# Two-layer perceiver kernel on one Trainium2 core: norm weights, value bias and attention denominator applied at a later point, four chunks of the last convolution as products on TensorE

## The chip, the cores and the metric

The kernel runs on one core of a Trainium2 chip. A core has a matrix engine (TensorE, PE in the profile), a vector engine (DVE), a scalar engine (ACT), GpSimd (POOL), and a queue for transfers (SyncE, SP). Each engine works through its own list of instructions in order, and waits on semaphores where it needs another engine's result. The metric is device time of one launch in microseconds (us); lower is better.

## The reference

The inputs are x (1×128×256), a context (1×12544×256) and a mask (1×128×12544). All arithmetic is float32. Cut to what is computed:

```python
# layer 0
x = x + xattn(layernorm(x), ctx, mask)       # 16 heads of 16, q, k, v with biases
#   scores = (q/4) @ k.T + (1-mask)*-10000; softmax; @ v
n = (x - mean) * rsqrt(var + 1e-5) * ln1_w + ln1_b
Q, K = elu(n @ q_w.T + q_b) + 1, elu(n @ k_w.T + k_b) + 1    # 64 features
V = n @ v_w.T + v_b
attn = causal(Q @ K.T) @ V / (causal(Q @ K.T) @ 1 + 1e-6)
# (then o_w, o_b, a residual, a norm with ln2_w and ln2_b, gelu FFN 256-1024-256)
# then an FFN with gate, 256-1024-256: activations rounded to 8 bits, weights to -1, 0, 1
# layer 1
x = x + (xattn(layernorm(x), ctx, no mask) @ Wo.T + bo)
# then an RWKV time mix (decay scan), and the last FFN:
h = bit_linear(norm(x), w1)                              # 128 x 1024
h = silu(conv3(h, conv_w) + conv_b)                      # per channel, 3 taps along the sequence
x = x + bit_linear(h, w2)
```

## The kernel before

The order of every engine is written out by hand. A layer's cross-attention goes over the context in NB = 14 blocks of TILES = 7 tiles of 128 keys. The 28 blocks are numbered m = 0 to 27; the program's step (m, t) is tile t of block m.

For each block TensorE makes the keys (`keys_in`, L1252, four units) and values (`values_in`, L1242), a rough maximum of the scores in bf16 (`maximum`, L1259, 32 products a block), the scores (L1315 brings in minus the maximum, L1319 the products of q and k), and the weighing of the values (`weigh`, L1337). In layer 0 DVE takes each maximum with the mask (L916) and adds the mask to half of a tile's scores (L977); ACT copies the other half to SBUF (`copy_second`, L652), POOL adds the mask there (`add_bias`, L500), and ACT takes the exponential of each (L659). In layer 1 there is no mask, ACT takes the exponential from PSUM (L664) and POOL is nearly idle.

The new running maximum of a block must come to rows before the next block's scores can use it: TensorE turns it (`turn_max`, L1354), and ACT copies it (`rows_out`, L638). This is done in the last step of a block, t = 6 (ROWS_AT). In steps like these `lent(m, t)` gives a product a bank of the scores' own: at t = 6 `turn_max` writes into a bank that is lent from the scores, ps_scores, which is free only when DVE has added the mask to it (L977); it stands behind the weighing and one pair of maxima, and ahead of the next unit of keys. In block 0, step 2, the small product L1487 uses the lent bank in the same way. How many maxima stand at each step comes from `count_at`, which bank each uses from the table MAX_BANK; `late_bank(m, t)` says at which steps of layer 0 the maximum behind the scores goes to ps_proj rather than ps_max.

Between the layers lies a part that I call the middle: end of the attention, first norm (L1067 to L1076), linear attention (L1082 to L1095), second norm (L1102, L1103), gelu FFN, the FFN with rounded weights, then the queries of layer 1 (L1008, L1011). While TensorE would wait for this chain, it makes keys and values of layer 1 (`between_in(u)`, whose units are the table BETWEEN). Where nothing is left, `idle_products` (L1409) and `idents` (L1413) are products with the identity whose result nobody reads. `turn` (L1227) turns a 128×256 tile in two products, ACT copies it out (L604), `project` (L1232) multiplies it by a weight. After layer 1 comes the tail: the division by the sum of weights (L1064), value bias (L1122), Wo, the RWKV part, and the last FFN, whose convolution runs over eight chunks of 128 channels. For each of seven chunks ACT makes the middle tap and bias (L811) and DVE adds the other two (L1201, L1205); POOL makes the eighth chunk alone (L569 to L576). ACT takes the silu of four chunks at a time (L818), TensorE turns them back (L1617), and DVE takes the largest absolute value of each row (L891).

## Time and profile before

| | us |
|---|---|
| median of 3 runs | 1025.69 (1024.63 to 1027.1) |
| profiled execution | 1025.05 |
| its span in the trace | 1023.3 |
| TensorE busy | 980.4 (96%) |
| DVE busy | 735.4 (72%) |
| ACT busy | 678.1 (66%) |
| POOL busy | 428.3 (42%) |

The span runs from the first to the last instruction that the trace shows; 1.75 us of the profiled execution's time lie around it. In a row of the timeline the two numbers at the front are the start and the time from it to the end of the group; "x4" counts records, and the bracket tells how long the engine had been idle before it and what released it. Matrix products are pipelined: one row's end can lie behind the next one's start.

### The profile page before, as it was taken

What the parts mean: (1) busy time and instruction counts of PE and PEld (TensorE: products, weight loads), DVE (VectorE), ACT (ScalarE), POOL (GpSimd) and SP (SyncE); (2) the same over time, 40 slices, a digit from 0 to 9 for tenths busy, and PEclk for the clock granted to TensorE, in tenths of its full rate; (3) what the DMA queues carried; (4) which work ended last, traced back from release to release, by engine and by line L of the source; (5) the groups of instructions that cost most, each with busy time, mean ns of one, the idle gap of its engine ahead of it and who ended that gap; (6) DMA issues with size and microseconds to landing.
All of it is one profiled execution on the core that took longest, in us unless ns stands there. A gap on an engine that the chain in (4) does not pass through costs nothing.

```text
span 1023.3 us, 30794 instructions
## 1 busy us (share of the span) xinstructions
PE 980.4 (96%) x12902; PEld 668.6 (65%) x12903; DVE 735.4 (72%) x1725; ACT 678.1 (66%) x963; POOL 428.3 (42%) x389
## 2 busy tenths in 40 slices
PE   8899999999999999999887899999999999999987
PEld 5466666666666666666564567767776667666665
DVE  5788888888888888887547866656566565666477
ACT  2777788787787878787554556566566665566652
POOL 4369888889888898884000000001000001000001
PEclk9999999999999999999999999999999999999999
DMA  8511122012211122014013010111101111000000
GB/s 326 145 54 34 62 74 74 20 56 74 74 40 40 70 75 74 2 56 163 12 50 146 2 38 2 37 38 38 38 2 38 38 37 38 2 3 2 2 2 6
DMA packets 14682, 53.31 MB, mean 52 GB/s; under 512 B 3024, under 2 KB 4816, under 8 KB 13648
## 3 DMA queue, kind: packets, MB, share of 16 engines
q1 hardware_dynamic: 14544, 51.35, 14.6%
q8 instruction: 102, 1.67, 0.7%
q14 instruction: 36, 0.29, 0.1%
HBM read 51.21 MB, written 0.13 MB: 50 GB/s over the span
## 4 chain that ended last, share of the span: by engine, by line
PE 85%; DVE 8%; issue 3%; ACT 3%; DMA 1%; SPq 0%; DVEq 0%; POOL 0%; ACTq 0%; POOLq 0%
PE ps_out L1337 17%; PE ps_scores L1319 16%; PE ps_proj L1252 15%; PE ps_proj L1242 13%; PE ps_max L1259 8%; PE ps_scores L1315 4%; PE ps_scores L1242 3%; ACT probs L664 2%; PE ps_scores L1348 1%; DVE unread L916 1%; DVE tile_max L919 1%; PE ps_scores L1252 1%; DMA ctx_t<-in_ctx_t 1%; PE ps_out L1242 1%; PE ps_scores L1354 0%
## 5 line engine op out<-in xcount | busy, mean ns | idle before, releaser
L919 DVE TENSOR_REDUCE tile_max<-ps_max 128x1 f32<-128x448 f32 x339 | 198.7, 619 | 142.1 <-PE ps_max L1259 134.6
L500 POOL TENSOR_TENSOR probs<-probs,masks 128x512 f32<-128x512 f32 x182 | 228.1, 1275 | 61.4 <-ACT probs L652 60.4
L916 DVE CUSTOM_DVE_ANT_0 unread<-ps_max,masks 128x448 bf16<-128x448 f32 x355 | 208.3, 620 | 62.8 <-PE ps_max L1259 61.9
L664 ACT ACTIVATE probs<-ps_scores 128x1024 f32<-128x1024 f32 x193 | 187.2, 1021 | 80.2 <-PE ps_scores L1319 80.1
L659 ACT ACTIVATE probs<-probs 128x1024 f32<-128x1024 f32 x196 | 206.9, 1056 | 40.3 <-DVE probs L977 34.3
L1319 PE MATMUL ps_scores<-q_pad,k_full 32*128 32x256 f32 x3088 | 231.5, 374 | 0.0
L1337 PE MATMUL ps_out<-probs,values 128*32 128x128 f32 x6272 | 215.4, 276 | 0.9 <-ACT probs L659 0.5
L1319 PEld LDWEIGHTS ps_scores<-q_pad,k_full 32*128 32x128 f32 x3088 | 193.2, 185 | 0.5
L1337 PEld LDWEIGHTS ps_out<-probs,values 128*32 128x32 f32 x6272 | 156.5, 109 | 56.2 <-issue 47.4
L1252 PE MATMUL ps_proj<-ctx_t,wk 128*128 128x448 f32 x388 | 171.0, 563 | 1.9 <-DVE tile_max L916 0.2
L1259 PE MATMUL ps_max<-k_high,q_high 32*128 32x448 bf16 x698 | 156.8, 356 | 6.9 <-DVE tile_max L919 4.3
L491 POOL CAST k_high<-k_full 128x896 bf16<-128x896 f32 x55 | 51.3, 934 | 245.1 <-ACT k_full L619 230.3
L1242 PE MATMUL ps_proj<-wv,ctx_t 128*128 128x256 f32 x600 | 145.7, 386 | 0.0
L1242 PEld LDWEIGHTS ps_proj<-wv,ctx_t 128*128 128x128 f32 x600 | 109.9, 190 | 20.2 <-DVE tile_max L919 3.0
L1259 PEld LDWEIGHTS ps_max<-k_high,q_high 32*128 32x128 bf16 x698 | 40.9, 91 | 125.7 <-issue 57.8
L977 DVE TENSOR_TENSOR probs<-ps_scores,masks 128x1024 f32<-128x1024 f32 x91 | 111.1, 1221 | 1.4 <-PE ps_scores L1319 1.4
L1315 PE MATMUL ps_scores<-max_rows,minus 32*128 32x512 bf16 x772 | 106.4, 380 | 4.8 <-ACT max_rows L638 1.7
L626 ACT COPY values<-ps_proj 128x512 f32<-128x512 f32 x75 | 43.9, 586 | 94.3 <-PE ps_proj L1242 94.2
L1252 PEld LDWEIGHTS ps_proj<-ctx_t,wk 128*128 128x128 f32 x388 | 65.8, 189 | 54.0 <-issue 36.3
L652 ACT COPY probs<-ps_scores 128x512 f32<-128x512 f32 x182 | 96.9, 586 | 0.2
L506 POOL TENSOR_TENSOR max_step<-max_wide 128x16 f32<-128x16 bf16 x30 | 7.3, 245 | 207.5 <-DVE max_wide L945 207.5
L619 ACT ACTIVATE k_full<-ps_proj,bk 128x448 f32<-128x448 f32 x97 | 60.9, 628 | 44.9 <-PE ps_proj L1252 44.9
(291 smaller groups left out, 953.3 us busy)
## 6 DMA issues: line engine op xcount, KB each, us to landing
ctx_t<-in_ctx_t SPq DMA_DIRECT2D x28, 896.0 KB, 5.3
masks<-in_mask_n SPq DMA_DIRECT2D x14, 448.0 KB, 3.5
masks<-in_mask_t SPq DMA_DIRECT2D x14, 448.0 KB, 3.6
room_w<-in_L_attn_f_w SPq DMA_DIRECT2D x2, 1024.0 KB, 7.2
room_w<-in_L_ffn_w SPq DMA_DIRECT2D x2, 1024.0 KB, 7.9
room_w<-in_L_ffn_w_gate SPq DMA_DIRECT2D x1, 1024.0 KB, 11.2
room_w<-in_L_ffn_w_up SPq DMA_DIRECT2D x1, 1024.0 KB, 13.6
room_w<-in_L_ffn_w_down SPq DMA_DIRECT2D x1, 1024.0 KB, 15.6
```

Of the source, the lines that this page charges most:

```text
L500: nc.gpsimd.tensor_tensor(p, p, three(mask_t[m % 2], TILES)[:, t, :].unsqueeze(1).to_broadcast([P, 4, P]), ALU.add).then_inc(sig("bias_add ...
L659: nc.scalar.activation(prob(T, half), prob(T, half), ACT.Exp).then_inc(sig(f"exp_done{half}"), 1)
L664: nc.scalar.activation(prob(T, half), scores_half(T, half), ACT.Exp).then_inc(sig(f"exp_done{half}"), 1)
L916: ins = v.tensor_tensor_reduce(unread[:, j % 2, :], max_bank(m, j)[:, 0:HALF], mask_n[m % 2][:, HALF * half:HALF * (half + 1)], 1.0, -3e38 ...
L919: ins = v.tensor_reduce(tile_max[:, h, half:half + 1], max_bank(m, j)[:, 0:HALF], AX_X, ALU.max)
L977: v.tensor_tensor(prob(T, 0).rearrange("p (h q) -> p h q", h=8), ps_scores[:, 0:2, :].rearrange("p a (h q) -> p (a h) q", q=P), three(mask ...
L1242: last = mm(bank[:, D * (t - at.start):D * (t - at.start + 1)], ctx_t[m % 3][:, c, P * t:P * (t + 1)], wv[l][:, c, :], start=(c == 0), sto ...
L1252: last = mm(bank[:, 0:HALF], wk[l][:, c, P * oc:P * (oc + 1)], ctx_t[m % 3][:, c, HALF * half:HALF * (half + 1)], start=(c == 0), stop=(c ...
L1259: mm(bank[:, 0:HALF], q_high[rows, c, zz, :], k_high[m % 2][rows, c, HALF * half:HALF * (half + 1)], start=True, stop=True).then_inc(sig(" ...
L1315: mm(banks[g], minus16[rows, :], max_rows[stage(m, t) % 2][rows, :], start=True, stop=True)
L1319: last = mm(banks[g][:, D * c:D * (c + 1)], k_full[m % 3][rows, c, P * t:P * (t + 1)], q_pad[rows, c, :], start=False, stop=True, skip_gro ...
L1337: last = mm(ps_out[VW * g:VW * (g + 1), P * c:P * (c + 1)], values[m % 2][:, t, h, :], prob(T, half)[:, P * o:P * (o + 1)], start=(in_stag ...
```

## The change

**Start.** The first context block comes in two halves with a semaphore each, and the query bias stands between them in SP's queue; the queries' product waits for its weights alone, and the first units of keys (`keys_in(0, 0)` and `(0, 1)`) for their half. `idents(4)` behind the queries' product is gone.

**End of a block in layer 0.** `turn_max` stands ahead of the weighing and writes into ps_proj; the step's maximum behind the scores goes to ps_max. ACT's `rows_out` stands ahead of `copy_second`. In block 0 one maximum moves from step 2 to step 5.

**Norms' weights and value bias.** They are loaded as columns (ten transfers) and applied to the turned tile. `turn_apart` turns the halves into two banks; DVE (`scaled`) writes the one and ACT (`turned_scaled`) the other, with scale and bias in the same instruction. The two DVE instructions behind each norm of the middle (L1075, L1076 and L1102, L1103) and the one ahead of Wo (L1122) are gone.

**Linear attention.** The numerator is copied undivided; the division stands behind the product with o_w, in one instruction with the addition. Bias is added to 128 of 384 columns first, and to V straight from PSUM. ACT's `between_out(3)` stands behind the copy of the turned features.

**Rounding and queries.** `ln_quant` has one reciprocal fewer ahead of the rounding. The bias of layer 1's queries is scaled in block 3, and two instructions from PSUM make the queries where there were three.

**Idle products.** Three become one at step (14, 0), and nine become two ahead of the last convolution.

**Last convolution.** Chunks 4 to 7 are twelve products with diagonal matrices of the taps, which POOL builds in blocks 17 to 20; ACT takes their silu from PSUM, a chunk at a time. Chunks 0 to 3 are as before, and POOL's chunk is gone.

The core of the diff:

```diff
         def late_bank(m, t):
-            return m < NB and (t >= LAST_AT or m > 0 and t == SUMS_AT)
+            return m < NB and (t == LAST_AT or m > 0 and t == SUMS_AT)
...
-                now = (2, 2, 2) if t < LAST_AT else (0, 2, 0) if t == LAST_AT else now
+                now = (1, 2, 2) if t == WEIGHTS_AT else (2, 2, 2) if t < LAST_AT else (1, 2, 0) if t == LAST_AT else now
...
+            def load_first_ctx(half):
+                cols = slice(HALF * half, HALF * (half + 1))
+                sp.dma_start(ctx_t[0][:, :, cols], a["ctx_t"][:, 0, :, cols]).then_inc(sig(f"first_ctx{half}"), 16)
...
             load_k_weights(0)
-            load_ctx(0)
+            load_first_ctx(0)
+            row(bq[0][:, :], "L0_xattn_bq", D, "q_bias0")
+            load_first_ctx(1)
             load_mask_n(0)
...
+            def scaled(k, w, b):
+                dve.wait_ge(sig("turned"), k)
+                v.tensor_scalar(xn_t[:, 0, :], ps_scores[:, 3, 0:P], w[:, 0:1] if w is not None else 1.0, b[:, 0:1], ALU.mult, ALU.add).then_inc(sig("first_scaled"), 1)
...
-                    link(v.tensor_scalar(xn[:, :], x1, stat[:, 6:7], stat[:, 32:33], ALU.subtract, ALU.mult))
-                    dve.wait_ge(sig("consts"), 16 * 13)
-                    link(v.tensor_tensor(xn[:, :], xn[:, :], lnw[:, 0, :], ALU.mult))
-                    out_(v.tensor_tensor(xn[:, :], xn[:, :], lnw[:, 1, :], ALU.add), "ln1_applied")
+                    out_(v.tensor_scalar(xn[:, :], x1, stat[:, 6:7], stat[:, 32:33], ALU.subtract, ALU.mult), "ln1_applied")
+                    scaled(2, ln1_w, ln1_b)
...
-                    link(v.tensor_scalar(stat[:, 16:17], ps_proj[:, D:D + 1], 1e-6, None, ALU.add))
+                    v.tensor_copy(tmp, ps_proj[:, 0:D]).then_inc(sig("lin_ready"), 1)
+                    out_(v.tensor_scalar(stat[:, 16:17], ps_proj[:, D:D + 1], 1e-6, None, ALU.add), "den_read")
                     link(v.reciprocal(stat[:, 17:18], stat[:, 16:17]))
-                    out_(v.tensor_scalar(tmp, ps_proj[:, 0:D], stat[:, 17:18], None, ALU.mult), "lin_ready")
                     link(v.tensor_tensor(a1, a0, b_o, ALU.add))
                     dve.wait_ge(sig("o_ready"), 1)
-                    link(v.tensor_tensor(a1, ps_proj[:, 0:D], a1, ALU.add))
+                    link(v.scalar_tensor_tensor(out=a1, in0=ps_proj[:, 0:D], scalar=stat[:, 17:18], in1=a1, op0=ALU.mult, op1=ALU.add))
...
+            def turn_apart(src):
+                for c in range(DC):
+                    last = tr((ps_scores[:, 3, 0:P], ps_max[:, 0, P:2 * P])[c], src[:, P * c:P * (c + 1)], ident[:, :])
+                return last
...
                         for k, j in behind_scores:
                             maximum(k, j)
+                        if rowed(m, t) and m < NB:
+                            proj_free(("max_copied", rowed(m, t) + 1))
+                            turn_max(rowed(m, t))
...
-            idle_products(9)
+            idle_products(2)
+            pe.wait_ge(sig("hidden_ready"), 2)
+            pe.wait_ge(sig("taps"), 3 * (FC - len(CONV_SPLIT)))
+            for c in range(len(CONV_SPLIT), FC):
+                for k in range(3):
+                    last = mm(tap_bank(c), tap(c, k), hp[:, c, k:P + k], start=(k == 0), stop=(k == 2))
+                last.then_inc(sig("pe_conv"), 1)
```

The order on TensorE at the end of a block of layer 0, before. L1259 is the maximum, L1315 and L1319 the scores of tile 6, L1337 the weighing of tile 5, L1354 the turn of the block's maximum, L1252 keys of the block after next:

```order
L1259 MATMUL ps_max<-k_high,q_high 128x448 x2
L1315 MATMUL ps_scores<-max_rows,minus 128x512 x4
L1319 MATMUL ps_scores<-q_pad,k_full 128x256 x8
L1259 MATMUL ps_proj<-k_high,q_high 128x448
L1337 MATMUL ps_out<-probs,values 32x128 x16
L1259 MATMUL ps_max<-k_high,q_high 128x448 x2
L1354 MATMUL ps_scores<-ident,max_wide 128x128 x4
L1252 MATMUL ps_proj<-ctx_t,wk 128x448 x2
```

The same place with the change (L1314, L1370, L1374, L1392, L1409 and L1307 are the same lines in the new text):

```order
L1314 MATMUL ps_max<-k_high,q_high 128x448 x2
L1370 MATMUL ps_scores<-max_rows,minus 128x512 x4
L1374 MATMUL ps_scores<-q_pad,k_full 128x256 x8
L1314 MATMUL ps_max<-k_high,q_high 128x448
L1409 MATMUL ps_proj<-ident,max_wide 128x128 x4
L1392 MATMUL ps_out<-probs,values 32x128 x16
L1314 MATMUL ps_max<-k_high,q_high 128x448 x2
L1307 MATMUL ps_proj<-ctx_t,wk 128x448 x2
```

The turn has moved ahead of the weighing and into ps_proj, and the single maximum behind the scores into ps_max.

ACT at the same place, before. L626 copies values, L659 is the exponential, L652 `copy_second`, L638 `rows_out`, L619 copies keys, L632 is the decay of the sums:

```order
L626 COPY values<-ps_proj 128x32x16
L659 ACTIVATE probs<-probs 128x1024
L652 COPY probs<-ps_scores 128x512 x2
L659 ACTIVATE probs<-probs 128x1024
L638 COPY max_rows<-ps_scores 128x512
L619 ACTIVATE k_full<-ps_proj,bk 128x448
L659 ACTIVATE probs<-probs 128x1024
L632 ACTIVATE decay<-max_step 128x16
```

And with the change:

```order
L643 COPY values<-ps_proj 128x32x16
L676 ACTIVATE probs<-probs 128x1024
L655 COPY max_rows<-ps_proj 128x512
L669 COPY probs<-ps_scores 128x512 x2
L676 ACTIVATE probs<-probs 128x1024
L636 ACTIVATE k_full<-ps_proj,bk 128x448
L676 ACTIVATE probs<-probs 128x1024
L649 ACTIVATE decay<-max_step 128x16
```

`rows_out` has moved ahead of the two copies that POOL's mask addition waits for.

TensorE at the last convolution, before. L1609 is the product with w1, L1409 idle products, L1617 the turn of the silu's result:

```order
L1609 MATMUL ps_scores<-xn_t,tern 128x128 x16
L1409 MATMUL ps_out<-wq,ident 128x256 x9
L1617 MATMUL ps_scores<-ident,masks 128x128 x4
L1409 MATMUL ps_out<-wq,ident 128x256
L1617 MATMUL ps_scores<-ident,masks 128x128 x4
```

And with the change:

```order
L1670 MATMUL ps_scores<-xn_t,tern 128x128 x16
L1464 MATMUL ps_out<-wq,ident 128x256 x2
L1679 MATMUL ps_scores<-masks,tern 128x128 x6
L1679 MATMUL ps_max<-masks,tern 128x128 x6
L1684 MATMUL ps_scores<-ident,masks 128x128 x4
L1464 MATMUL ps_out<-wq,ident 128x256
L1684 MATMUL ps_scores<-ident,masks 128x128 x4
```

Twelve products with the tap matrices stand where seven of nine idle products stood.

## Rows read from the trace of the kernel before

**Rows 1.** The page, part 1: busy time of each engine.

```profile
PE 980.4 (96%) x12902; PEld 668.6 (65%) x12903; DVE 735.4 (72%) x1725; ACT 678.1 (66%) x963; POOL 428.3 (42%) x389
```

**Rows 2.** Windows, tail: length; busy us of each engine; clock; DMA share; GB/s.

```profile
1000.00:1023.30 23.30, 17.13 (x99) 12.75 (x97) 16.06 (x45) 7.39 (x15) 3.20 (x6) 0.96 0.02 6
```

**Rows 3.** The start: chain piece, bias issue, timeline, durations of the key products.

```profile
3.11 6.76 DMA ctx_t<-in_ctx_t
...
bk<-in_L_xattn_bk SPq DMA_DIRECT2D x1, 1.0 KB, 4.7
...
10.01 2.23 PE L1252 MATMUL ps_scores<-ctx_t,wk 128*128 128x448 f32 x4 [0.40 <-DMA ctx_t<-in_ctx_t]
...
L1252 PE MATMUL ps_scores<-ctx_t,wk x20: 539/539/1087, 10.0 to 33.7; 128*128 128x448 f32 x20
```

**Rows 4.** Timeline of TensorE, block 0, step 2.

```profile
50.82 0.36 PE L1487 MATMUL ps_scores<-small,ones 128*128 128x3 f32 x2 [1.17 <-DVE probs L977]
```

**Rows 5.** Waits of TensorE from 60 to 480; timeline, turn at two block ends.

```profile
PE ps_scores L1354 <- DVE probs L977: 3.1, 13, 0.6
...
400.36 0.36 PE L1259 MATMUL ps_max<-k_high,q_high 32*128 32x448 bf16 x2
...
400.92 0.40 PE L1354 MATMUL ps_scores<-ident,max_wide 128*128 128x128 bf16 x4 [0.20 <-DVE probs L977]
401.46 1.77 PE L1252 MATMUL ps_proj<-ctx_t,wk 128*128 128x448 f32 x4
...
466.38 0.40 PE L1354 MATMUL ps_scores<-ident,max_wide 128*128 128x128 bf16 x4 [0.30 <-DVE probs L977]
466.62 1.72 PE L1252 MATMUL ps_proj<-ctx_t,wk 128*128 128x448 f32 x4
```

**Rows 6.** Timeline of ACT, POOL and TensorE behind the block end.

```profile
400.18 2.50 POOL L500 TENSOR_TENSOR probs<-probs,masks 128x512 f32<-128x512 f32 x2 [0.41 <-ACT probs L652]
...
401.86 0.57 ACT L638 COPY max_rows<-ps_scores 128x512 bf16<-128x512 bf16 x1
...
403.80 1.05 ACT L659 ACTIVATE probs<-probs 128x1024 f32<-128x1024 f32 x1
...
408.04 1.06 ACT L659 ACTIVATE probs<-probs 128x1024 f32<-128x1024 f32 x1
...
408.64 1.16 PE L1337 MATMUL ps_out<-probs,values 128*32 128x128 f32 x32
```

**Rows 7.** Timeline of the middle, DVE, POOL and TensorE.

```profile
496.17 0.94 POOL L491 CAST k_high<-k_full 128x896 bf16<-128x896 f32 x1 [18.09 <-ACT k_full L619]
496.33 1.05 DVE L1076 TENSOR_TENSOR xn<-xn,lnw 128x256 f32<-128x256 f32 x1
...
497.52 0.41 PE L1227 MATMUL ps_max<-ident,xn 128*128 128x128 f32 x2 [0.36 <-DVE xn L1076]
...
505.28 0.44 PE L1227 MATMUL ps_max<-ident,room_t 128*128 128x128 f32 x2 [0.18 <-DVE room_t L1095]
...
510.47 0.44 PE L1227 MATMUL ps_max<-ident,xn 128*128 128x128 f32 x2 [0.15 <-DVE xn L1103]
```

**Rows 8.** Timeline of the tail.

```profile
983.08 0.42 DVE L1122 TENSOR_TENSOR xn<-probs,bv 128x256 f32<-128x256 f32 x1
...
990.47 2.94 PE L1588 MATMUL ps_scores<-room_t,room_w 128*128 128x128 f32 x24 [0.55 <-DVE room_t L1146]
...
1008.54 2.80 ACT L811 ACTIVATE masks<-masks,small 128x128 f32<-128x128 f32 x7 [1.51 <-DVE masks L1195]
...
1009.15 1.42 DVE L1201 SCALAR_TENSOR_TENSOR masks<-masks,small 128x128 f32<-128x128 f32 x4
...
1010.49 1.40 DVE L1205 SCALAR_TENSOR_TENSOR masks<-masks,small 128x128 f32<-128x128 f32 x4
...
1012.61 0.66 PE L1617 MATMUL ps_scores<-ident,masks 128*128 128x128 f32 x4 [0.51 <-ACT masks L818]
...
1015.14 0.69 DVE L891 TENSOR_REDUCE stat<-ps_scores 128x1 f32<-128x512 f32 x1 [0.81 <-PE ps_scores L1617]
```

184 lines of the change are left out of this document (109 added, 75 removed).

## The prediction, made before the changed kernel was timed

> **What bounds the kernel now.** I read the busy times first: TensorE is busy 96% of the span [rows 1]. So an edit pays only where TensorE stands idle or where it leaves out TensorE's work, and I looked for both with the list of TensorE's waits and the timeline. In layer 0 from 60 to 480 us, the wait that recurs is that of the block maximum's turn, 3.1 us over 13 block ends, for the mask addition by DVE that frees its bank [rows 5]. The other idle places are the start, where TensorE waits for the first context block [rows 3]; the middle, where each turn of a tile waits a little for DVE [rows 7]; and the tail, where nothing but idle products is left to fill in and the chain runs through DVE and ACT [rows 8]. In flow, a product starts about 0.16 before the modelled end of the row ahead: 466.38 with 0.40 ends at 466.78, and the next row starts at 466.62 [rows 5]. So a wait that goes gives its bracket and up to 0.16 more.
>
> **Start.** The first context block is issued at 3.11 and lands 6.76 later, at 9.87; the keys' bias lands at 2.64 + 4.7 = 7.34, and TensorE starts the keys at 10.01 [rows 3]. 896 KB came in between 3.11 and 9.87, most of it behind the bias; with half the bytes, issued at the same place, I put the landing midway in the stretch that starts at 7.34 and halves what is left (8.6), at 8.1, and the keys at 8.2, 1.8 earlier. The second half lands as the whole did, about 9.9, and is needed only for the second unit. The query bias then lands with it and is read by DVE while TensorE makes keys. Not all of the 1.8 stays: at this place one key product took 1087 ns, where the median is 539 [rows 3], twice the time, so the lower of the clock's two levels was still on for one record after the engine had been through its idents and the queries' product. If the level rises at the same moment as before (about 11.0), an earlier start puts two or three records into the slow stretch, each 0.55 more: 1.8 - 1.5 × 0.55 = **-0.95**. Bounds: one slow record as before, -1.8; six slow records, 1.8 - 5 × 0.55, that is +0.95. The Trainium skill, page "TensorE: Matmul & The Clock Gate", says that the clock falls back without activity; `idents(4)` was such activity, and its absence speaks for the upper bound.
>
> **Block 0.** TensorE waits 1.17 at the product of step 2 for the mask addition [rows 4]. One maximum fewer on DVE ahead of it (0.55, from one maximum of DVE following the other) takes 0.55 off; the product itself is made at step 5 at about 0.27 of TensorE: **-0.3** (0 to -0.85).
>
> **Block ends.** At 400.92 the turn starts 0.56 after the pair of maxima ahead of it, and the keys 0.54 after the turn; in flow the latter is 0.24 (466.38 to 466.62) [rows 5], and ahead of the turn its bracket of 0.20 and a part of the 0.16 are lost, say 0.27. So 0.27 + 0.30 = 0.57 go per block end, and the move takes them out, since in its new place the turn writes to a free bank. But I don't credit that. The edit also puts `rows_out` (0.57 [rows 6]) ahead of ACT's two copies. It can't begin before the turn is through and must end before the first copy, which I estimate at 0.9 of delay; POOL's mask addition (2.50 for both heads' halves) starts at 401.1 in place of 400.18 [rows 6], and ends at 403.6. The exponential at 403.80 reads its result, so it can start only 0.18 earlier than before. From there ACT has no gap of size up to the exponential at 408.04, which ends at 409.10, and the second half of the weighing that starts at 408.64 (408.64 + half of 1.16 = 409.2 [rows 6]) reads that. TensorE there was only 0.1 behind ACT. So the 0.57 end in a new wait of about 0.4 at the weighing of the next tile, and 0.2 stay: 13 × 0.2 = **-2.6**. Bounds: nothing stays, 0; all but 0.12 (the maximum behind the scores now waits for its bank in ps_max) stays, 13 × 0.45 = -5.9.
>
> **Step (14, 0).** Two idle products fewer, but the maxima behind them wait for DVE anyway: **-0.15** (0 to -0.5).
>
> **Middle.** (1) First norm: two DVE instructions go; the turn at 497.52 waited 0.36 for the second of them [rows 7]. Without them the tile is ready before TensorE has ended its unit of values, so the bracket and the 0.16 of flow go, 0.52. The pass out of PSUM now is a 128×128 instruction with scale and bias on each of two engines; ACT takes 2.80/7 = 0.40 for such a one [rows 8], 0.03 more than its plain copy of the whole, and TensorE waits for two engines: -0.46. (2) The bias on 128 columns in place of 384 is hidden by the values that TensorE makes then; ACT's copy behind the turned features gives 0.1. (3) The division: two one-column instructions and one of 256 columns become one copy of 256. TensorE waited only 0.18 for it (505.28 [rows 7]), so at most 0.34 go. The addition behind the product gets a multiplication, 0.06 more. (4) Second norm: again two DVE instructions of 0.42 to 0.46 each, but the turn waited for them only 0.15 (510.47 [rows 7]), so 0.31 at most, less 0.03. (5) One reciprocal less ahead of the rounding, 0.1; three query instructions become two, 0.2. Sum 0.46 + 0.1 + 0.34 - 0.06 + 0.28 + 0.3 = **-1.4** (-0.8 if neither flow nor ACT's share comes; -1.8 if TensorE's units also move up). What is late next is TensorE itself, in its units of keys and values.
>
> The second norm instruction took 1.05 and ended just as POOL's cast, 496.17 with 0.94, had [rows 7]; a like one in the tail takes 0.42 [rows 8]. With the change the tile's ready signal comes earlier and three such casts stand beside `scaled` and the instructions behind it. If each could be blocked like this, 0.6 would come back: I keep it in the upper bound. The Trainium skill, page "SBUF — State Buffer", section "Who interferes with whom", states that a DVE instruction with two SBUF inputs contends with a GpSimd instruction that reads SBUF, and one with at most one SBUF input does not, outside the two-port modes. The row agrees for the first part; by the second `scaled`, which reads PSUM, would be free of it.
>
> **Tail.** The value bias (0.42 [rows 8], and 0.04 to the next) goes from the path and the pass gets 0.03 longer: -0.4. Rounding, -0.1. Convolution: before, ACT's seven middle taps start at 1008.54, DVE ends the first four chunks at 1010.49 + 1.40 = 1011.89, ACT's silu follows and the first turn starts at 1012.61; the second half goes through DVE and silu once more, and its reduction starts at 1015.14 [rows 8]. After: the twelve products need both halves of the hidden tile (there when DVE starts L1201, 1009.15 [rows 8]); at 2.94/24 = 0.1225 a record and two records each [rows 8] they end at 1012.1. ACT takes silus 4 and 5 before 1011.9, then the first half (0.63), then 6 and 7 at 0.3 to 0.4 each, to 1013.3. The turn of the second half follows right behind the first (0.7 each), and the reduction starts at 1014.0: -1.1. The first half stays where it was, so more isn't to be had. **-1.6** (-1.0 to -2.0). Twelve taps on POOL at 0.6 each lie in layer 1, where it is idle. The chain behind (reduction, rounding, last product) is as before.
>
> **Sum.** 0.95 + 0.3 + 2.6 + 0.15 + 1.4 + 1.6 = 7.0. The profiled execution would take 1025.05 - 7.0 = 1018.05 (span 1016.3); it lies 0.64 under the median of the runs, so the forecast is 1025.69 - 7.0 = **1018.7**.
>
> **Rivals.** All with the other terms as above.
> (B) ACT's chain isn't as tight as I read it, and a block end gives 0.42: 13 × 0.22 = 2.9 more, 1015.8. For it: POOL waited 0.41 before the addition at 400.18, so there is slack in that chain [rows 6]. Against it: the exponential at 403.80 starts right when ACT gets to it.
> (C) Block ends give nothing, or the clock at the start stays low and eats 1.9: 1018.7 + 2.6 = 1021.3, or 1020.6. In the tail the clock is already 0.96 on average [rows 2]; where it falls because nine idle products become two, the products of the convolution cost twice, 2.9 more, but hide half of it.
> (D) Slower. The delay of POOL's mask addition (0.9 per block end) passes through exp, weighing and scores' banks to TensorE in full, at each of 13 ends: +11.7 in place of -2.6, so 1025.69 + 11.7 - 4.4 = 1033.0. It makes the kernel slower as soon as more than 4.4/13 = 0.34 per end gets through. Against it: POOL waited 0.41 there before [rows 6], and TensorE's gain of 0.57 is a cushion.
> (E) The change doesn't do what it says: the halves' two passes wait on each other, casts on POOL block DVE (+0.6 at each norm), the turn in ps_proj delays the keys behind `rows_out`. Then 7.0 shrinks under 2: about 1024.5.
>
> **Numbers.** My forecast 0.58 (1016.8 to 1020.4), B 0.17, C 0.14, D 0.06, E 0.05. The range takes A, B and C with the start's and the middle's bounds: 1013.8 to 1022.8, and leaves D, E and the far ends out. What a measurement can tell from no change is about 0.2%, 2.05 us. Faster than 1023.6: A, B and most of C, 0.86. Within: E and the rest of C, 0.08. Slower than 1027.7: D, 0.06.
>
> **What would show it.** Start: first key product at 8.2, with two or three records of 1.09. Block ends: turn without a wait, keys right behind the maxima, and a wait of about 0.4 of the first or second weighing for the exponential; POOL's mask addition 0.9 later. Middle: turns at 497.0, 504.4 and 509.3 less what came before, with TensorE in its units ahead of them. Tail: reduction of the second half 1.1 nearer to the hidden tile, twelve products in 3.0. Wrong I would be, above all, if the block period (from the turn at 400.92 to the next block's) grew, or shrank by over 0.4.

## Result

The changed kernel takes 1020.43 us (median of 4 runs, 1018.68 to 1020.71), the kernel before 1025.8 (4 runs). The ratio is 0.9946, 95% interval 0.9931 to 0.996. So it is 5.4 us faster, where 7.0 were forecast; 1018.7 was the forecast time, and the range 1013.8 to 1022.8 holds the result.

The profiled execution took 1020.71, with a span of 1019.0. TensorE is busy as long as in [rows 1], 980.6 (96%); DVE has 731.8 and POOL 432.1, within 4 us of what they had. Part 2 of the page shows a change in its row of the granted clock, a single 8 behind the middle of the span:

```profile
PEclk9999999999999999999998999999999999999999
```

To see where time was won and lost, I set each step's start (its first L1315, now L1370: the product that brings in the maximum) beside that of the kernel before. The lead is start before minus start after. Sums by stretch, with the lead at the end of each:

| stretch | forecast | changed kernel's profile | lead at its end |
|---|---|---|---|
| start, to step (0, 0) | 0.95 | 1.24 | 1.24 |
| block 0 | 0.3 | 0.48 | 1.72 |
| 13 block ends | 2.6 | 13 ends 2.94, then the step behind the last one gives 0.88 back | 4.44 (step (13, 0)), 3.56 (step (13, 1)), block 3 taken in |
| blocks 3 and 4, beside their ends | not foreseen | -0.25 | 2.66 (step (5, 0)) |
| middle, to step (14, 0) | 1.4 | 1.59 | 5.14 |
| steps (14, 0) to (15, 0) | 0.15 | -2.55 | 2.59 |
| layer 1 to block 27 | 0 | 0 | 2.59 |
| tail | 1.6 | 1.7 | 4.3 |

Five terms came out within 0.35 us of their size, the block ends before the loss behind the last one. What was missed above all is one stretch, in which half of the lead is lost. Its window rows (stretch, length, busy of TensorE, granted clock, DMA share, GB/s) in the changed kernel:

```profile
548.50:551.90 3.40, 3.35 (x36) 0.50 0.00 0
551.90:555.40 3.50, 2.44 (x45) 0.99 0.00 0
555.40:558.80 3.40, 3.40 (x50) 0.51 0.02 5
```

A granted clock of 0.50 is the lower of TensorE's two levels (1.2 GHz), 1.00 the higher (2.4 GHz). In the kernel before, whose step (14, 0) starts 5.1 later:

```profile
549.00:557.00 8.00, 6.72 (x91) 1.00 0.18 73
557.00:565.00 8.00, 6.38 (x109) 1.00 0.00 0
```

So in the changed kernel the clock fell to its lower level twice, from 548.5 to 551.9 and from 555.4 to 558.8 (the first expectation below has both 2 us too early). The timeline of TensorE there, changed kernel:

```profile
546.96 0.36 PE L1314 MATMUL ps_max<-k_high,q_high 32*128 32x448 bf16 x1 [0.17 <-DVE tile_max L949]
547.25 0.70 PE L1464 MATMUL ps_out<-wq,ident 128*128 128x256 f32 x2
548.02 0.36 PE L1314 MATMUL ps_max<-k_high,q_high 32*128 32x448 bf16 x1
...
549.03 2.21 PE L1374 MATMUL ps_scores<-q_pad,k_full 32*128 32x256 f32 x16
```

Sixteen records of scores take 2.21, where such a group takes 1.20 at the high level (at 332.43 in the kernel before, shown further on). The first low stretch begins 1.3 us behind the place where the change took out two idle products: the one that is left is the row at 547.25.

### The profile page after: what moved, and what is told of

Read it like the earlier page. It is cut to its first block, busy times and chain, and to the rows that moved or that the text cites. A ratio compares the mean times of both kernels' runs of the same rounds, so it can differ in the third digit from the quotient of the medians.

```text
span 1019.0 us, 30805 instructions
## 1 busy us (share of the span) xinstructions
PE 980.6 (96%) x12901; PEld 668.0 (66%) x12901; DVE 731.8 (72%) x1719; ACT 679.2 (67%) x963; POOL 432.1 (42%) x396
## 4 chain that ended last, share of the span: by engine, by line
PE 86%; DVE 6%; ACT 3%; issue 3%; DMA 1%; SPq 0%; POOL 0%; DVEq 0%; POOLq 0%; ACTq 0%
PE ps_out L1392 17%; PE ps_scores L1374 16%; PE ps_proj L1307 15%; PE ps_proj L1294 13%; PE ps_max L1314 8%; PE ps_scores L1370 4%; PE ps_scores L1294 3%; ACT probs L681 2%; PE ps_scores L1403 1%; DVE tile_max L949 1%; PE ps_scores L1307 1%; DMA bq<-in_L_xattn_bq 1%; PE ps_out L1294 1%; PE ps_out L1307 1%; PE ps_proj L1279 0%
## 5 line engine op out<-in xcount | busy, mean ns | idle before, releaser
L946 DVE CUSTOM_DVE_ANT_0 unread<-ps_max,masks 128x448 bf16<-128x448 f32 x367 | 214.6, 619 | 59.8 <-PE ps_max L1314 58.7
L1374 PE MATMUL ps_scores<-q_pad,k_full 32*128 32x256 f32 x3088 | 233.1, 376 | 0.0
L1392 PE MATMUL ps_out<-probs,values 128*32 128x128 f32 x6272 | 218.5, 277 | 1.3 <-ACT probs L676 0.8
L1374 PEld LDWEIGHTS ps_scores<-q_pad,k_full 32*128 32x128 f32 x3088 | 194.4, 186 | 0.5
L1392 PEld LDWEIGHTS ps_out<-probs,values 128*32 128x32 f32 x6272 | 156.7, 110 | 57.1 <-issue 44.0
L1307 PE MATMUL ps_proj<-ctx_t,wk 128*128 128x448 f32 x388 | 171.1, 563 | 0.2 <-DVE tile_max L946 0.2
L1314 PE MATMUL ps_max<-k_high,q_high 32*128 32x448 bf16 x710 | 161.8, 357 | 7.6 <-DVE tile_max L949 4.2
L1314 PEld LDWEIGHTS ps_max<-k_high,q_high 32*128 32x128 bf16 x710 | 42.1, 91 | 129.5 <-issue 58.0
L1370 PE MATMUL ps_scores<-max_rows,minus 32*128 32x512 bf16 x772 | 106.7, 381 | 4.8 <-ACT max_rows L655 1.7
L1307 PEld LDWEIGHTS ps_proj<-ctx_t,wk 128*128 128x128 f32 x388 | 65.8, 189 | 52.9 <-issue 40.6
```

Source lines behind the costliest of these rows:

```text
L946: ins = v.tensor_tensor_reduce(unread[:, j % 2, :], max_bank(m, j)[:, 0:HALF], mask_n[m % 2][:, HALF * half:HALF * (half + 1)], 1.0, -3e38 ...
L1307: last = mm(bank[:, 0:HALF], wk[l][:, c, P * oc:P * (oc + 1)], ctx_t[m % 3][:, c, HALF * half:HALF * (half + 1)], start=(c == 0), stop=(c ...
L1314: mm(bank[:, 0:HALF], q_high[rows, c, zz, :], k_high[m % 2][rows, c, HALF * half:HALF * (half + 1)], start=True, stop=True).then_inc(sig(" ...
L1370: mm(banks[g], minus16[rows, :], max_rows[stage(m, t) % 2][rows, :], start=True, stop=True)
L1374: last = mm(banks[g][:, D * c:D * (c + 1)], k_full[m % 3][rows, c, P * t:P * (t + 1)], q_pad[rows, c, :], start=False, stop=True, skip_gro ...
L1392: last = mm(ps_out[VW * g:VW * (g + 1), P * c:P * (c + 1)], values[m % 2][:, t, h, :], prob(T, half)[:, P * o:P * (o + 1)], start=(in_stag ...
```

## Experiments

Every kernel was timed in five rounds beside the kernel before. "Lead" always means against the profile of the kernel before, at the start of the step named. The mean granted clock of each execution is listed with its time; it shows how many executions had low stretches, while where they lay is seen only in the profiled one. Single executions of one kernel differ by 1.5 us and more, and the longer ones mostly have the lower mean clock, so the leads of the profiles tell small terms apart that the medians don't. A profile is one execution, though, and where the clock falls and when it first rises differs from one to the next. The experiments ran on four chips; what compares across them is the ratio to the kernel before, which was timed beside each.

### The idle products: after_idle3 and before_idle1

after_idle3:

```diff
                         if (m, t) == (NB, 0):
-                            idle_products(1)
+                            idle_products(3)
```

> The changed kernel with three idle products again at step (14, 0), all else as changed. In the changed kernel's profile the granted clock fell to the low level twice right behind this step (546.5 to 549.9 and 553.3 to 556.7 us), and the lead over the kernel before went from 5.14 us at step (14, 0) to 2.59 at step (15, 0). Theory: the two idle products that were left out let the clock fall, so with them the lead stays near 5.0 at (15, 0), the profile shows no low stretch there, and the time is about 2.4 us lower, 1018.0. Rival: the clock falls there because of what stands ahead (the middle, shorter by 1.6 us, has less TensorE work between waits); then the low stretches stay and the time is 1020.4 plus 0 to 0.3.

Measured: 1019.3 us (6 runs), ratio 0.9937, interval 0.9925 to 0.9949. In its profile the lead stays: 5.61 at (14, 0), 5.61 at (15, 0), and the clock is high from 9.8 us to the end:

```profile
553.00:557.00 4.00, 3.44 (x63) 1.00 0.01 4
```

Two executions had a mean clock of 1.0 and took 1017.76 and 1017.87; three with 0.998 took 1019.3 to 1019.6, one with 0.997 took 1021.0. The changed kernel had three at 0.997 (1020.3 to 1020.7) and one at 0.998 (1018.68). So the median fell by 1.1, not by 2.4, and the intervals of the two ratios overlap. If the products prevent the falls, they do it in a part of the executions only; a later kernel with three of them (after_turn_first) has both low stretches in its profile.

before_idle1 is the same edit the other way, in the kernel before (3 to 1).

> The kernel before with one idle product instead of three at step (14, 0), nothing else changed. Theory: the clock falls behind this step here too, and the kernel becomes 2.0 to 2.6 us slower, about 1028. Rival: in the kernel before, the fall needs the rest of the change as well; then the time is 1025.7 less 0 to 0.2.

Measured: 1026.3 us (12 runs), ratio 1.0006, interval 0.9997 to 1.0015. The profile shows what the theory said: the lead goes from 0.35 at (14, 0) to -2.08 at (15, 0), behind the place of the two products:

```profile
553.00:557.00 4.00, 3.83 (x49) 0.60 0.02 4
557.00:561.00 4.00, 2.68 (x43) 0.93 0.00 0
561.00:565.00 4.00, 3.64 (x45) 0.62 0.00 0
```

But the median moved by only 0.95 against the 17 executions of the kernel before that were timed with it, and the interval holds 1: a slower kernel isn't shown. The kernel before seems to have such stretches itself: of the 72 executions listed beside the experiments, 20 had a mean clock of 0.999 (median 1024.66) and 25 had 0.996 (median 1026.45). At 0.996 or less were 30 of these 72, and ten of the twelve of before_idle1. The rival, that the fall needs the rest of the change, is out, since the profile has the fall without it. What decides in which execution it comes isn't shown; the counts speak for the two products making it rarer.

### ACT's order at a block end: after_rows_between

On top of after_idle3:

```diff
                 for k in range(2):
+                    if k == 1 and rows:
+                        rows_out(rows)
                     nc.scalar.copy(prob(T, 1)[:, 512 * k:512 * (k + 1)], ps_scores[:, 2 + k, :]).then_inc(sig("scores_copied"), 1)
...
-                            if rowed(m, t):
-                                rows_out(rowed(m, t))
-                            copy_second(T)
+                            copy_second(T, rowed(m, t))
```

> The kernel of after_idle3 with ACT's rows_out between the two copies of copy_second, where the changed kernel has it ahead of both. POOL adds the mask half by half (1.25 us each), so it can start on the first half at once, and the second copy still comes within those 1.25. Theory: the copy ahead of both delays POOL, then the exponential, then the weighing, and this holds each block end of layer 0 to a gain of 0.22 to 0.30 where 0.57 were free, and loses 0.88 at the last one (from step (13, 0) to (13, 1)); without the delay the block period falls from 32.67 to between 32.3 and 32.5, and the last end gives 0.9: 3 to 5 us less than after_idle3, 1013 to 1015. Rival: what holds the block ends is something else (TensorE's keys wait for rows_out, since both use ps_proj, or the bank of the maximum ahead), then only the last end's 0.9 is gained, about 1017.1, or nothing.

Measured: 1017.96 us (5 runs), ratio 0.9924, interval 0.9911 to 0.9937, 1.3 less than after_idle3; executions with the same mean clock differ by 0.8 to 1.2 (1.0: 1016.76 and 1016.99 against 1017.76 and 1017.87; 0.998: 1018.2 against 1019.3, the middle ones of three each). In the profiles the last end gives 0.7 of it: between (13, 0) and (13, 1) after_idle3 loses 0.87 of its lead, this kernel 0.17. The other ends give 0.30 in place of 0.22, together 0.8 from (0, 6) to (13, 0), so the period is 32.6, not 32.3 to 32.5: the theory was right on the last end and too high on the others. (This profile's start is 0.8 behind that of after_idle3, which is why the sum of 1.5 doesn't show in its span.) The chain at the last end, changed kernel:

```profile
461.22 0.58 ACT L655 COPY max_rows<-ps_proj 128x512 bf16<-128x512 bf16 x1
...
461.70 1.08 ACT L669 COPY probs<-ps_scores 128x512 f32<-128x512 f32 x2
...
462.37 2.50 POOL L514 TENSOR_TENSOR probs<-probs,masks 128x512 f32<-128x512 f32 x2 [1.45 <-ACT probs L669]
...
464.96 1.50 POOL L483 TENSOR_SCALAR masks<-masks 128x384 f32<-128x384 f32 x1
...
466.49 2.35 DVE L1018 TENSOR_TENSOR probs<-ps_scores,masks 128x1024 f32<-128x1024 f32 x2 [4.31 <-POOL masks L483]
...
467.75 2.19 ACT L676 ACTIVATE probs<-probs 128x1024 f32<-128x1024 f32 x2 [0.44 <-DVE probs L1018]
```

and after_rows_between:

```profile
461.14 2.50 POOL L514 TENSOR_TENSOR probs<-probs,masks 128x512 f32<-128x512 f32 x2 [0.86 <-ACT probs L671]
...
465.26 2.36 DVE L1018 TENSOR_TENSOR probs<-ps_scores,masks 128x1024 f32<-128x1024 f32 x2 [3.74 <-POOL masks L483]
...
466.52 2.19 ACT L678 ACTIVATE probs<-probs 128x1024 f32<-128x1024 f32 x2 [0.18 <-DVE probs L1018]
```

With `rows_out` ahead of both copies POOL stands idle 1.45 instead of 0.86, and everything that follows it on POOL comes 0.6 later, counted from step (12, 6): the mask addition, then the scaling of the mask that DVE needs for block 13. At the other ends TensorE has keys and values to make. Here its timeline has none between 463.8 and 470.6, and it stands idle for 1.16 ahead of the scores at 467.82. That the keys and values cover the delay elsewhere is read from this; no run tests it alone.

### The block ends alone: before_block_ends

The kernel before with `turn_max`, `late_bank` and `rows_out` as in the change, nothing else.

> The kernel before with the block ends alone as changed: turn_max ahead of the weighing and in ps_proj, the single maximum behind the scores in ps_max, rows_out ahead of copy_second. Theory, from the steps of the changed kernel: each end gains 0.29 from the scores of step 6 to those of the next block and loses 0.07 in the step behind it, 12 x 0.22 = 2.6; the last one, into block 13, loses 0.6 to 0.9 instead, since that block gives TensorE no keys or values to do; sum 1.8 to 2.0 less by the end of layer 0, so 1023.5. Rival: the last end's loss belongs to another part of the change (columns' loads, the scaled bias); then the lead at the end of layer 0 is 2.6 to 2.9.

Measured: 1023.8 us (11 runs), ratio 0.9981, interval 0.9972 to 0.9991. Its lead grows from 0.38 at (0, 6) to 0.68 at (1, 0) and then by 0.22 a block to 3.29 at (13, 0), and falls to 2.42 at (13, 1). So 13 ends give 2.9, the step behind the last gives 0.87 back, block 3 keeps its length (0.22 is gained over it as over any other), and the rival is out. This profile has two low stretches, 37.9 to 41.3 and one from 556.7 on, though three idle products stand at (14, 0). Its keys started at 9.08, its clock had risen early (at 7.2), and the 1.44 of lead that it had at (0, 0) were 0.39 at (0, 2), behind the first low stretch. Where the 0.57 of the prediction went is seen in one end of the changed kernel; ahead, the same in the kernel before:

```profile
332.43 1.20 PE L1319 MATMUL ps_scores<-q_pad,k_full 32*128 32x256 f32 x16
333.29 0.35 PE L1259 MATMUL ps_proj<-k_high,q_high 32*128 32x448 bf16 x1
333.57 1.08 PE L1337 MATMUL ps_out<-probs,values 128*32 128x128 f32 x32
334.58 0.36 PE L1259 MATMUL ps_max<-k_high,q_high 32*128 32x448 bf16 x2
335.15 0.40 PE L1354 MATMUL ps_scores<-ident,max_wide 128*128 128x128 bf16 x4 [0.21 <-DVE probs L977]
335.68 1.77 PE L1252 MATMUL ps_proj<-ctx_t,wk 128*128 128x448 f32 x4
```

```profile
329.17 1.20 PE L1374 MATMUL ps_scores<-q_pad,k_full 32*128 32x256 f32 x16
...
329.52 0.62 DVE L946 CUSTOM_DVE_ANT_0 unread<-ps_max,masks 128x448 bf16<-128x448 f32 x1 [0.26 <-PE ps_max L1314]
...
330.21 0.36 PE L1314 MATMUL ps_max<-k_high,q_high 32*128 32x448 bf16 x1
330.50 0.40 PE L1409 MATMUL ps_proj<-ident,max_wide 128*128 128x128 bf16 x4
...
330.83 1.08 PE L1392 MATMUL ps_out<-probs,values 128*32 128x128 f32 x32
...
331.84 0.36 PE L1314 MATMUL ps_max<-k_high,q_high 32*128 32x448 bf16 x2
...
332.14 1.77 PE L1307 MATMUL ps_proj<-ctx_t,wk 128*128 128x448 f32 x4
```

Read by starts: maxima to turn 0.57, turn to keys 0.53 before; maxima to keys 0.30 and turn to weighing 0.33 after, which is 0.47 less. The single maximum now starts 1.04 behind the scores instead of 0.86, because its bank in ps_max is still being read by DVE (the row at 329.52, which ends at 330.14): 0.18 back. That makes 0.29 at the end itself, and a further 0.07 go at the next step.

### The turn ahead of the maximum: after_turn_first

On top of after_bias_in_middle (below), `turn_max` stands ahead of the single maximum.

> The kernel of after_bias_in_middle with the turn of the block maximum ahead of the single maximum of step 6 instead of behind it. In the changed kernel that maximum starts 1.04 us after the scores (329.17 to 330.21) where the kernel before needed 0.86 (332.43 to 333.29), since its bank in ps_max must be read by DVE first. Theory: this wait of 0.18 is why a block end gives 0.29 and not 0.47; the turn (0.33) in its place covers it, the step from 6 to the next block's 0 becomes 4.90 - 0.18 = 4.72, the block period 32.4, and the time falls by 13 x 0.18 = 2.3 to about 1015.8. Rival: DVE then takes the maximum later and its mask addition and all behind it move back with it, so the weighing of the next step waits instead, and nothing changes.

Measured: 1021.33 us (11 runs), ratio 0.9962, interval 0.9949 to 0.9974. This is 3.2 more than without the edit; the ratios, 0.9962 and 0.9925, are apart beyond their intervals, and the leads of the two profiles at (14, 0) are 3.93 and 7.16. Behind (14, 0) this profile has two low stretches, in spite of three idle products, which take its lead to 0.99 at (15, 0). The step from 6 to the next block takes 5.20, as in the kernel before (5.19). The profile of it:

```profile
330.09 1.20 PE L1374 MATMUL ps_scores<-q_pad,k_full 32*128 32x256 f32 x16
...
331.22 0.40 PE L1409 MATMUL ps_proj<-ident,max_wide 128*128 128x128 bf16 x4
...
331.55 0.36 PE L1314 MATMUL ps_max<-k_high,q_high 32*128 32x448 bf16 x1
331.84 1.08 PE L1392 MATMUL ps_out<-probs,values 128*32 128x128 f32 x32
...
331.94 0.62 DVE L946 CUSTOM_DVE_ANT_0 unread<-ps_max,masks 128x448 bf16<-128x448 f32 x1 [0.33 <-PE ps_max L1314]
```

The rival holds: DVE now stands idle 0.33 for the later maximum. And the turn starts 1.13 behind the scores, not 0.86: the single maximum, which takes 32 rows as the scores do, started while they were still running (333.29, where their end is put at 333.63), and the turn on 128 rows starts about when they end (331.22 for 331.29). The 0.18 couldn't be covered in this way.

### What holds block 3: before_middle and after_bias_in_middle

before_middle is the kernel before with norm weights, value bias, denominator, rounding and the queries of layer 1 as in the change.

> The kernel before with norm weights, value bias, denominator, rounding and the queries of layer 1 alone as changed (with the columns' loads and the scaled query bias in block 3). Start, block ends, idle products and convolution are as before. Theory: +0.6 in block 3, where DVE is what the step waits for and the scaling of the bias (0.69 us beside a POOL instruction that reads SBUF) stands in its list; -1.6 in the middle; -0.5 in the tail; sum -1.5, 1024.0. Rival: the 0.6 in block 3 comes from something else (then block 3 keeps its length), and the middle's gain goes into falls of the clock (then the profile shows low stretches and the time is within 0.5 of before).

Measured: 1022.25 us (11 runs), ratio 0.9972, interval 0.996 to 0.9983. That is 3.1 less than the kernel before, where 1.5 were expected. The profile bears out the terms, as follows; the rest may lie in part in the clock, since nine of the 11 executions had a mean clock of 0.999 or 1.0, and of the kernel before 21 of 72. Why low stretches are rarer here isn't shown. Lead 0.37 at (3, 0), -0.23 at (4, 0), 0.11 from (5, 0) on: 0.6 lost in block 3, of which 0.35 come back in block 4, whose end has the longest wait of the 13 in [rows 5] in the kernel before (0.55, at 203.59) and 0.20 here. Net -0.26. From (13, 6) to (14, 0) the lead grows by 1.58. In this profile one low stretch behind (14, 0) takes 1.4 of it, in spite of three idle products; the tail gives 0.4. DVE in block 3 of this kernel:

```profile
152.00 1.24 DVE L1064 TENSOR_TENSOR x<-x,bv 128x256 f32<-128x256 f32 x1
...
152.92 2.09 POOL L481 TENSOR_SCALAR room_w<-room_w 128x512 f32<-128x512 f32 x1
...
153.16 0.69 DVE L1066 TENSOR_SCALAR bq<-bq 128x256 f32<-128x256 f32 x1
153.78 0.61 DVE L930 CUSTOM_DVE_ANT_0 unread<-ps_max,masks 128x448 bf16<-128x448 f32 x1
...
154.45 0.36 PE L1291 MATMUL ps_max<-k_high,q_high 32*128 32x448 bf16 x1 [0.67 <-DVE tile_max L930]
```

The scaling of the bias stands between TensorE and a maximum that it waits for. after_bias_in_middle moves that line (on top of after_rows_between) to where DVE waits for the gelu FFN:

```diff
                         if (m, t) == (BIAS_AT, 2):
...
-                            dve.wait_ge(sig("q_bias1"), 16)
-                            v.tensor_scalar(bq[1][:, :], bq[1][:, :], HD ** -0.5, None, ALU.mult).then_inc(sig("q_bias_scaled"), 1)
...
+                    dve.wait_ge(sig("q_bias1"), 16)
+                    v.tensor_scalar(bq[1][:, :], bq[1][:, :], HD ** -0.5, None, ALU.mult).then_inc(sig("q_bias_scaled"), 1)
                     dve.wait_ge(sig("f2_ready"), 1)
```

> The kernel of after_rows_between with the scaling of the query bias of layer 1 moved from block 3 into the middle, where DVE waits some 10 us for the gelu FFN. Theory: block 3 loses its 0.6, nothing is paid for it in the middle: 1017.4 where after_rows_between has 1018.0. Rival: what holds block 3 is the addition of the value bias ahead of it, which stays, and nothing changes.

Measured: 1018.09 us (5 runs), ratio 0.9925, interval 0.9912 to 0.9938: no difference to 1017.96 that the medians could tell. In the profile block 3 now gains 0.30 like the others, and from (0, 6) to (13, 0) the lead grows by 3.68, against 3.42 in after_rows_between: 0.26, not 0.6, because the 0.35 of block 4 go with it. Its fastest run, with a mean clock of 1.0, took 1015.99; those of after_rows_between took 1016.76 and 1016.99.

### The convolution alone: before_conv

> The kernel before with the last convolution alone as changed: twelve products with diagonal taps, built by POOL in blocks 17 to 20, silu chunk by chunk, two idle products ahead of it instead of nine. Theory: no step up to block 27 moves, and the end comes 1.1 us earlier, all of it between the hidden tile and the reduction of the second half: 1024.3. Rival: the taps on POOL hold up layer 1, or the products run at the low clock level (twice 2.9 us) since seven idle products are gone: then the gain is 0 to 0.4.

Measured: 1024.25 us (12 runs), ratio 0.9984, interval 0.9971 to 0.9998. That is 1.1 less than the kernel before, as expected. No step moves up to block 27 (leads of 0.02 to 0.12), so POOL's taps cost nothing. The span is 1022.1, 1.2 shorter. Its rows answer to [rows 8]:

```profile
1009.14 1.60 PE L1623 MATMUL ps_scores<-masks,tern 128*128 128x128 f32 x12
...
1010.58 1.50 PE L1623 MATMUL ps_max<-masks,tern 128*128 128x128 f32 x12
...
1011.64 0.63 ACT L822 ACTIVATE masks<-masks 128x512 f32<-128x512 f32 x1 [0.49 <-DVE masks L1210]
...
1012.33 0.66 PE L1628 MATMUL ps_scores<-ident,masks 128*128 128x128 f32 x4 [0.24 <-ACT masks L822]
...
1013.89 0.69 DVE L897 TENSOR_REDUCE stat<-ps_scores 128x1 f32<-128x512 f32 x1 [0.18 <-PE ps_scores L1628]
```

The products end at 1012.1 as forecast, at the high level, and the second reduction starts 1.25 earlier (1013.89 for 1015.14; 1.1 forecast). The 0.15 more are DVE's: its second set of taps ended at 1011.6 instead of 1011.9. The four took 1.14 here (at 1010.47) and 1.40 in the kernel before ([rows 8]), where POOL worked on its chunk beside them; DVE's last three there, made when POOL had ended, took 0.87, about 0.29 each as here. So what the change gave there is most likely that POOL's chunk is gone, and the prediction had no term for it.

### The start: after_bias_ahead and after_bias_second

after_bias_ahead is after_idle3 with SP's row for the query bias of layer 0 ahead of the first half of the context.

> The kernel of after_idle3 with the query bias loaded ahead of the first half of the context instead of behind it. In the changed kernel's profile the first keys start at 7.50, but the turn of the queries waits 1.56 us for DVE, which waited for the bias until 9.76. Theory: the bias is now the last thing that the start waits for; ahead of the half it lands about 8, the turn of the queries starts about 9.3 instead of 10.80, the keys start 0 to 0.4 later, and the time is 1.0 to 1.4 us lower than after_idle3. Rival: the start is then held by the next thing (second half of the context, first mask), which landed about 9.9 to 11 in the kernel before; then 0 to 0.5.

Measured: 1021.97 us (5 runs), ratio 0.9963, interval 0.9951 to 0.9974, so 2.7 worse than after_idle3, against both theories. The rows that answer to [rows 3], from the timeline of the changed kernel, then of after_bias_ahead:

```profile
7.50 1.74 PE L1307 MATMUL ps_scores<-ctx_t,wk 128*128 128x448 f32 x4 [0.47 <-DMA ctx_t<-in_ctx_t]
...
9.76 0.42 DVE L1039 TENSOR_TENSOR room_t<-ps_proj,bq 128x256 f32<-128x256 f32 x1 [4.48 <-DMA bq<-in_L_xattn_bq]
...
10.80 0.66 PE L1490 MATMUL ps_max<-ident,room_t 128*128 128x128 f32 x4 [1.56 <-DVE room_t L1046]
```

```profile
10.28 3.32 PE L1307 MATMUL ps_scores<-ctx_t,wk 128*128 128x448 f32 x4 [2.38 <-DMA ctx_t<-in_ctx_t]
```

The bias took 6.6 and 6.3 from issue to landing, and the half that stands behind it let the keys start 2.8 later than in the changed kernel and 2.6 later than in after_idle3 (7.73), whose half stands ahead of it. Besides, TensorE stood idle 2.38, its keys then ran at the low level (3.32), and this profile has a low stretch from 40.9 to 44.3, which took another 1.1 of lead.

after_bias_second is after_turn_first with the bias right behind the queries' weights.

> The kernel of after_turn_first with the query bias of layer 0 loaded right behind the queries' weights, as in the kernel before, and the context's halves behind both. In the changed kernel the turn of the queries waits for this bias (until 9.76); loaded just ahead of the first half it held that half up until 10.2 instead (after_bias_ahead). Theory: its 128 short rows take transfer time out of proportion to their 128 KB wherever they stand, but at this place they go while the engine still waits for x and wq; the first half lands at 8.5 to 9, the turn of the queries starts by 10.3 without waiting, 0.3 to 0.7 earlier. Rival: whatever stands behind the bias comes later by what the bias takes (2 us or more), so the keys start as late as in the kernel before (10.0) and the start's whole gain is gone: +1.2.

Measured: 1021.54 us (8 runs), ratio 0.9961, interval 0.9947 to 0.9975; after_turn_first 1021.33. Neither theory: the keys start at 7.78 and nothing waits for the bias, but the keys take 2.87 at the low level, and the turn of the queries starts at 10.48. The lead at step (0, 2) is 1.62, against 1.59 of after_turn_first. So in these profiles the transfer of the bias (128 rows of 1 KB) held the keys up by 2.6 at one place and by nothing at another; why is left open.

### The falls of the clock again, and all together: after_idle_between and after_combined

One more idle product at (14, 0), ahead of the third maximum, where TensorE waits 0.77 for DVE (545.90 in the changed kernel); after_idle_between has it on top of after_turn_first.

```diff
-                        for k, j in behind_scores:
+                        for i, (k, j) in enumerate(behind_scores):
+                            if (m, t, i) == (NB, 0, 2):
+                                idle_products(1)
                             maximum(k, j)
```

> The kernel of after_turn_first with one more idle product at step (14, 0), ahead of the third maximum, where TensorE waits 0.77 us for DVE. Theory: the low stretches at step (14, 0) hang on the share of time that TensorE stands idle there, so with it fewer executions show a mean clock under 0.999, and the median falls by 0.5 to 1.4 while the fastest runs stay as they are. Rival: they hang on something that idle products don't reach; then the spread and the median are as in after_turn_first.

Measured: 1020.24 us (6 runs), ratio 0.995, interval 0.9933 to 0.9968; 1.1 under after_turn_first. Four of its six executions had a mean clock of 1.0, of after_turn_first's one in 11; the fastest took 1019.56, that of after_turn_first 1019.68. This is as the theory said. The counts over all kernels with the changed start and middle point the same way: a mean clock of 1.0 had none of four executions with one idle product, 6 of 40 with three, and 7 of 11 with four (here and in after_combined). A mean clock is lowered by a low stretch anywhere, so these counts aren't of step (14, 0) alone.

> The kernel of after_bias_in_middle (three idle products at (14, 0), rows_out between the two copies, query bias scaled in the middle, the turn behind the maximum as in the changed kernel) with the fourth idle product of after_idle_between at step (14, 0). Theory: the fastest runs stay at 1016.0, where after_bias_in_middle has its one with a mean clock of 1.0, and most runs now lie there, so the median is 1016.2 to 1017.2, below the changed kernel's 1020.4 and below after_bias_in_middle's 1018.1. Rival: the low stretches come back in other places; then the median is about 1018 as without it.

Measured: 1016.45 us (5 runs), ratio 0.9916, interval 0.99 to 0.9932. This is in the range of the theory, though its interval overlaps that of after_bias_in_middle. Three of five executions had a mean clock of 1.0 (1015.84 to 1016.45). Lead 7.15 at (14, 0) and the same at (15, 0). This version is 9.2 us faster than the kernel before, timed beside it, and 4.0 below the median of the changed kernel (ratios 0.9916 and 0.9946); its edits take out no work: they move `rows_out` and a scaling, and put three idle products in.

## Why the prediction was right, point by point

**Start.** Size about right (0.95; 1.24 in the profile, and in six other profiles with this start 1.04 to 1.81, where four with the start of before differed by 0.1 to 0.4 at step (0, 2) from the profile before themselves), reason wrong. The first half landed by 7.5, not at 8.1: it was issued at 2.64, 0.47 ahead of the 3.11 that the prediction kept, since the bias no longer goes ahead of it. The two or three key products at the low level weren't there in this execution: the clock was up before. The bias landed at 9.7, near where I had it, but the step by which it is read while TensorE makes keys failed: the keys had ended at 9.24, and TensorE waited 1.56 for what came of the bias. Where the clock rose late (after_idle3, at 9.8), the keys took 2.70 and lasted until the bias had gone through DVE, so slow keys cost nothing there; the lead was greater because the bias was read at 9.35 instead of 9.76. The later of the two, keys and bias, sets the time, and the prediction had a price for the keys alone. Besides, its 1.8 - 1.5 × 0.55 is 0.98, not 0.95.

**Block 0.** 0.48 for 0.3. DVE gave the 0.55 that I took; steps 4 to 6, with the product at step 5, cost 0.06 and not 0.27.

**Block ends.** 0.22 an end, as forecast, but by another sum. I had 0.57 free and 0.4 eaten by ACT and POOL. In truth 0.47 were free, since the turn costs 0.33 in flow; 0.18 went at the maximum's bank, for which I had 0.12 only in a bound, and 0.07 went through ACT and POOL. What I had for ACT's order (about 0.4) was five to six times too much at twelve ends, and too little at the last: there it cost 0.88, of which after_rows_between gives 0.7 back. So a right total from wrong terms, which is luck in part. The last end is rival D's mechanism, with D's chain (copy, POOL, DVE, exponential, scores), at the one place where TensorE has no keys and values to make.

**Block 3.** The prediction gave the scaling of the bias no term at all. It was named in the change and costed at nothing, with no cover named; before_middle shows 0.61 at once and 0.26 net.

**Middle.** 1.59 for 1.4. The turns come where TensorE's units end, as forecast (497.0, 504.3 and 509.1 when the lead of 3.55 is added, for 497.0, 504.4 and 509.3); the last row below, of the second norm, has no wait for DVE left where [rows 7] has 0.15. `scaled` took 0.41 beside POOL's three casts (2.69), and 0.41 at the second norm with no cast beside it, so the 0.6 of rival E weren't there. The Trainium skill, page "SBUF — State Buffer", section "Who interferes with whom", says that a DVE instruction with at most one SBUF input, outside the two-port modes, does not contend with GpSimd; these rows agree. They agree on the other part too: two instructions with one SBUF input and an SBUF output, of a form which that section lists as able to enter such a mode, took 0.72 (L1122, beside the casts) and 0.69 (the bias in block 3) where 0.41 is usual.

```profile
492.35 2.69 POOL L505 CAST k_high<-k_full 128x896 bf16<-128x896 f32 x3 [19.59 <-DVE xn L1118]
...
493.94 0.41 DVE L887 TENSOR_SCALAR xn_t<-ps_scores,small 128x128 f32<-128x128 f32 x1 [1.67 <-PE ps_max L1274]
...
494.46 0.72 DVE L1122 TENSOR_SCALAR room_t<-x,stat 128x256 f32<-128x256 f32 x1
...
505.57 0.27 PE L1274 MATMUL ps_scores<-ident,xn 128*128 128x128 f32 x1
```

**Step (14, 0).** The failed step: -0.15 was forecast, with "the maxima behind them wait for DVE anyway". That is so: the two idle products had cost 0.1 (lead 5.14 at (14, 0), 5.24 at (14, 1)). What they bought was left out. In the profile the low stretches cost 2.65 (from 5.24 to 2.59 at (15, 0)), in the median about 1.1 (after_idle3 against the changed kernel, whose intervals overlap). That TensorE's clock falls there is shown; that the idle products hold it up rests on two pairs of profiles and on the counts above, and three of them did not always do it. I had weighed the clock at the start and in the tail, where the change also removes idle products, and not here, where TensorE works in short pieces between DVE's maxima and is idle between them (6.38 of 8 us busy in the kernel before). Between the forecast 7.0 and the measured 5.4 lie 1.6 us, and this is the largest part of them.

**Tail.** 1.7 for 1.6; convolution 1.2 (1.1), value bias and rounding 0.4 (0.5). The prediction feared for the clock here because of the mean of 0.96 in [rows 2]; that mean comes from the last 1.9 us of the span, behind the convolution, and the products of the convolution ran at the high level.

**Sum.** Without the low stretches the profiled lead would be 6.9, by luck next to 7.0: the last end and block 3, 1.1 together, were made up by start, block 0, ends and middle, each a little better than its term.

## What to carry to other kernels

An idle product that waits beside another engine's work costs next to nothing (0.1 us for two here), and just there it may be part of what keeps the clock up: before taking it out for its 0.5 us, look at how busy TensorE is around it, and time several executions, for the clock falls in some of them only. Where an engine's order is changed at a place that repeats, look at the last repetition apart: what covered the delay twelve times wasn't there the thirteenth. And an instruction that moves off a chain has a new place; name whom it holds up there, even where it is small.

## Not expected of the hardware

One low stretch behind step (14, 0) costs 1.2 to 1.6 us, at a place where TensorE is busy 6.4 to 6.7 of 8 us in the kernel before and never idle for as long as 1 us at a time. With one idle product there it came twice in both profiled kernels; with three it came in five of ten profiles, once in four of them and twice in after_turn_first; with four in neither of two. The kernel before had it, or the like of it elsewhere, in many of its own executions (mean clock 0.996 in 25 of 72), and two profiles have a low stretch between 37.9 and 44.3 us. A product on 32 rows starts 0.27 earlier behind the scores than one on 128 rows (0.86 against 1.13). And 128 KB for the query bias, loaded ahead of the context's half, let the keys that read that half start 2.6 us later.
